# Key sums of an attention block: per-unit accumulators filled by adding DMAs, and a shared ring of PSUM banks

## The reference

```python
scores = jnp.einsum('bhsd,bhtd->bhst', q, k) / math.sqrt(HEAD_DIM)
scores = scores + _band_mask(S, scores.dtype)   # 0.1 where |s - t| <= 2
attn = jax.nn.softmax(scores, axis=-1)
out = jnp.einsum('bhst,bhtd->bhsd', attn, v)
```

## Time and profile before

| | |
|---|---|
| median of 3 runs | 4730.73 us (4729.35 to 4734.55) |
| the profiled execution, its own time | 4733.77 us |
| its span, first to last instruction | 4731.9 us |
| busy share of PE, DVE, POOL, ACT | 98%, 71%, 60%, 52% |
| mean granted clock of PE | 0.987 |
| attention stage, about | 670 to 4283 us |

### The profile page before, as it was taken

One profiled execution on the slowest core, in us unless ns is written; L12 is line 12 of the kernel. 1 busy time (PEld: TensorE's weight loads), 2 busy tenths in 40 slices (PEclk: granted clock), 3 DMA queues, 4 the chain that ended last, 5 costly groups with the idle time before them and its releaser, 6 DMA issues. The chain is left out here.

```text
span 4731.9 us, 68176 instructions
## 1 busy us (share of the span) xinstructions
PE 4630.4 (98%) x24976; PEld 2572.3 (54%) x24976; DVE 3346.7 (71%) x5663; ACT 2446.4 (52%) x4652; POOL 2820.4 (60%) x2207
## 2 busy tenths in 40 slices
PE   7999989999999999999999999999999999996999
PEld 6888844444444444444444444444444444434777
DVE  6444477777777777777777777777777777744776
ACT  2222226666666666666666666666666666661211
POOL 2111037777777777777777777777777777780000
PEclk9999979999999999999999999999999999998999
DMA  7655531112121212121212112111212121104443
GB/s 253 212 202 201 197 89 37 50 48 54 41 58 36 61 31 63 32 61 43 57 39 53 50 41 53 41 50 49 54 42 58 36 61 31 30 15 174 166 158 118
DMA packets 250862, 372.60 MB, mean 79 GB/s; under 512 B 36545, under 2 KB 103105, under 8 KB 245442
## 3 DMA queue, kind: packets, MB, share of 16 engines
q1 hardware_dynamic: 250562, 368.66, 26.2%
HBM read 211.82 MB, written 156.24 MB: 78 GB/s over the span
## 5 line engine op out<-in xcount | busy, mean ns | idle before, releaser
L699 DVE TENSOR_REDUCE part_max<-ps_m 128x1 f32<-128x512 f32 x4096 | 2547.8, 683 | 842.4 <-PE ps_m L595 840.6
L770 POOL TENSOR_TENSOR pair<-p_sb 128x512 f32<-128x512 f32 x2048 | 2565.9, 1283 | 920.6 <-ACT p_sb L687 597.0
L687 ACT ACTIVATE p_sb<-ps_s 128x512 f32<-128x512 f32 x4096 | 2114.8, 603 | 1288.4 <-PE ps_s L615 1225.2
L615 PE MATMUL ps_s<-q_st,k_st 97*128 97x512 f32 x4096 | 1728.5, 424 | 6.8 <-ACT p_sb L687 6.8
L595 PE MATMUL ps_m<-k_st,q_st 96*128 96x512 f32 x4096 | 1636.8, 403 | 21.6 <-POOL k_st L762 20.1
L615 PEld LDWEIGHTS ps_s<-q_st,k_st 97*128 97x128 f32 x4096 | 773.0, 189 | 1010.8 <-ACT p_sb L687 452.0
L629 PE MATMUL ps_o<-p_sb,v_sb 128*32 128x512 f32 x8192 | 1090.7, 605 | 0.0
L595 PEld LDWEIGHTS ps_m<-k_st,q_st 96*128 96x128 f32 x4096 | 786.2, 192 | 186.3 <-DVE part_max L699 29.2
L639 PE MATMUL ps_d<-pair,ones 128*32 128x512 f32 x4096 | 534.0, 593 | 3.8 <-POOL pair L770 3.8
L629 PEld LDWEIGHTS ps_o<-p_sb,v_sb 128*32 128x32 f32 x8192 | 161.3, 108 | 349.9 <-ACT p_sb L687 295.4
L166 POOL TENSOR_TENSOR xb<-xin,bo_row 128x2048 f32<-128x2048 f32 x16 | 75.5, 4716 | 428.1 <-DMA xin<-in_x 417.3
(11 more groups left out here) (93 smaller groups left out, 2631.9 us busy)
## 6 DMA issues: line engine op xcount, KB each, us to landing
q_st<-q_hi_d SPq DMA_DIRECT2D x128, 256.0 KB, 4.2
k_st<-k_hi_d SPq DMA_DIRECT2D x128, 256.0 KB, 4.9
xin<-in_x SPq DMA_DIRECT2D x16, 1024.0 KB, 8.4
xb_d<-xb SPq DMA_DIRECT2D x16, 1024.0 KB, 5.1
q_hi_d<-s_hi SPq DMA_DIRECT2D x64, 256.0 KB, 2.0
q_lo_d<-s_lo SPq DMA_DIRECT2D x64, 256.0 KB, 2.3
k_hi_d<-s_hi SPq DMA_DIRECT2D x64, 256.0 KB, 2.3
k_lo_d<-s_lo SPq DMA_DIRECT2D x64, 256.0 KB, 2.6
```

What stands on the lines that cost most here:

```text
L615: nc.tensor.matmul(ps_s[:, (HG * s + h) % RING_S, :], k_st[0:ROWS + 1, unit // QC % 2, kt // TT, h, kt % TT * P:(kt % TT + 1) * P], q_st[0 ...
L687: nc.scalar.activation(p_sb[:, s % SLOTS, h, :], ps_s[:, (HG * s + h) % RING_S, :], ACT.Exp, scale=SCALE).then_inc(p_ready, 1)
L699: nc.vector.tensor_reduce(part_max[:, unit % 2, col, n:n + 1], ps_m[:, seq % RING_M, :], AX.X, ALU.max).then_inc(max_taken, 1)
L770: nc.gpsimd.tensor_tensor(pair[:, m % PAIR_RING, h, :], p_sb[:, s % SLOTS, h, :], p_sb[:, (s + 1) % SLOTS, h, :], ALU.add).then_inc(paired, 1)
```

## The change

Key sums are no longer accumulated by PE for every macro. SBUF holds two accumulators (`acc`, even and odd macros) for each of two units. POOL writes the first two pair sums of a unit straight into them, one instruction of 2048 columns a macro. For each of the six later macros it adds the odd step's slot of `p_sb` to the even step's slot in place (so it first waits for that step's product with V), waits for its own result, and issues a DMA that adds the slot to the accumulator (`accum_op=ALU.add`, 1 MB). The two DMA semaphores are `merged[0]` and `merged[1]`. PE multiplies ones with the two accumulators once a unit (`add_keys(unit)`, behind step 6 of the next unit), into a bank of the maxima's ring. That ring gets the fourth bank, the former `ps_d`; `free_bank`, `max_place`, `turn_place` and `sum_place` compute whose bank is reused. The products with V of two steps now follow each other, behind each even step. ACT may overwrite an even slot only once its macro's DMA has landed. Band products of step s-1 now come behind the second take of step s, `copy_sum` before step 7, `o_high` before step 13, POOL's `scale_o` and `o_low` behind macros 4 and 5, and the SyncE chain at steps 7, 8, 10 and 11.

```diff
-    RING_S, RING_M = 3, 3
+    RING_S, RING_M = 3, 4
-    PAIR_RING = 4
+    MERGES = PAIRS // 2 - 1
+    SUM_AT = 6
+    SUM_AFTER = HG * (SUM_AT + LEAD + 1)
...
+    def sums_before(unit, j):
+        return max(unit - 2 + (j >= SUM_AFTER), 0)
+    def max_place(unit, j):
+        return max_no(unit, j) + sums_before(unit, j)
+    def sum_place(unit):
+        return max_place(unit + 2, SUM_AFTER) - 1 if unit < NU - 2 else MAXES * NU + NU + unit
+    def merges_to(m):
+        return MERGES * (m // PAIRS) + m % PAIRS // 2
...
-        pair = sb("pair", [P, PAIR_RING, HG, CH])
+        acc = sb("acc", [P, 2, 2, HG, CH])
...
         @block.sync
-                        if kt == 4:
+                        if kt == 7:
                             store_sum(unit - 1)
-                        if kt == 6:
+                        if kt == 8:
                             load_den(unit - 1)
-                        if kt == 9:
+                        if kt == 10:
                             store_rec(unit - 1)
...
         @block.tensor
+            def free_bank(place):
+                old = place - RING_M
+                if old in sum_places:
+                    pe.wait_ge(sum_copied, sum_places[old] + 1)
+                else:
+                    at_least(pe, max_taken, old + 1 - sums_to[max(old, 0)])
+                return place % RING_M
...
+            def add_keys(unit):
+                bank = free_bank(sum_place(unit))
+                for n in range(2):
+                    pe.wait_ge(merged[n], 16 * MERGES * (unit + 1))
+                    for h in range(HG):
+                        last = nc.tensor.matmul(ps_m[h * HD:(h + 1) * HD, bank, :], ones[:], acc[:, unit % 2, n, h, :],
+                                                start=(n == 0), stop=(n == 1))
                 last.then_inc(sum_done, 1)
...
-                if 2 <= s < ST + 2:
+                if s % 2 == 0 and 2 <= s < ST + 2:
                     weigh(s - 2)
-                if s >= 4 and s % 2 == 1:
-                    add_keys(s // 2 - 2)
+                    weigh(s - 1)
+                if s >= KT and s % KT == SUM_AT:
+                    add_keys(s // KT - 1)
...
         @block.scalar
-                if kt == 4 and unit > 0:
+                if kt == 7 and unit > 0:
                     copy_sum(unit - 1)
-                if kt == 14 and unit > 0:
+                if kt == 13 and unit > 0:
                     o_high(unit - 1)
                 if s >= SLOTS:
+                    old = (s - SLOTS) // 2
                     act.wait_ge(pv_done, s - SLOTS + 1)
-                    act.wait_ge(paired, HG * ((s - SLOTS) // 2 + 1))
+                    act.wait_ge(paired, old + 1)
+                    if s % 2 == 0 and old % PAIRS > 1:
+                        act.wait_ge(merged[old % 2], 16 * merges_to(old))
...
         @block.vector
             for m in range(NM):
-                if m > 0:
-                    spread_band(2 * m - 1)
                 for s in (2 * m, 2 * m + 1):
                     for h in range(HG):
                         ahead(*max_at(s, h))
-                spread_band(2 * m)
+                        if h == 1 and s > 0:
+                            spread_band(s - 1)
...
         @block.gpsimd
-                at_least(pool, sum_done, m - PAIR_RING + 1)
-                for h in range(HG):
-                    nc.gpsimd.tensor_tensor(pair[:, m % PAIR_RING, h, :], p_sb[:, s % SLOTS, h, :],
-                                            p_sb[:, (s + 1) % SLOTS, h, :], ALU.add).then_inc(paired, 1)
+                unit, n = m // PAIRS, m % PAIRS
+                p_even, p_odd, total = p_sb[:, s % SLOTS], p_sb[:, (s + 1) % SLOTS], acc[:, unit % 2, n % 2]
+                if n < 2:
+                    at_least(pool, sum_done, unit - 1)
+                    nc.gpsimd.tensor_tensor(total, p_even, p_odd, ALU.add).then_inc(paired, 1)
+                else:
+                    pool.wait_ge(pv_done, s + 1)
+                    nc.gpsimd.tensor_tensor(p_even, p_even, p_odd, ALU.add).then_inc(paired, 1)
+                    at_least(pool, merged[n % 2], 16 * (merges_to(m) - 1))
+                    pool.wait_ge(paired, m + 1)
+                    pool.dma_start(total, p_even, accum_op=ALU.add).then_inc(merged[n % 2], 16)
-                if m % PAIRS == 5 and m > PAIRS:
+                if n == 4 and unit > 0:
-                    scale_o(m // PAIRS - 1)
+                    scale_o(unit - 1)
```

More of the change, by code:

```diff
@@ L439, in attend @@
     scored, p_ready, banded, paired = sem("scored"), sem("p_ready"), sem("banded"), sem("paired")
+    merged = [sem(f"merged{i}") for i in range(2)]
     pv_done, sum_done, o_copied, sum_copied, o_out, sum_out = (
@@ L453, in attend, with max_no, turn_no, turn_place @@
     bands_to = list(itertools.accumulate(int(near(s) is not None) for s in range(ST)))
-    def max_seq(unit, j):
+    def max_no(unit, j):
         return MAXES * unit + j + (unit - 1 + (j >= TURN_AFTER) if unit else 0)
-    def turn_seq(unit):
+    def turn_no(unit):
         return MAXES * (unit + 1) + unit + (TURN_AFTER if unit < NU - 1 else 0)
+    def sums_before(unit, j):
+        return max(unit - 2 + (j >= SUM_AFTER), 0)
+    def max_place(unit, j):
+        return max_no(unit, j) + sums_before(unit, j)
+    def turn_place(unit):
+        return turn_no(unit) + (sums_before(unit + 1, TURN_AFTER) if unit < NU - 1 else NU - 2)
+    def sum_place(unit):
+        return max_place(unit + 2, SUM_AFTER) - 1 if unit < NU - 2 else MAXES * NU + NU + unit
+    sum_places = {sum_place(unit): unit for unit in range(NU)}
+    sums_to = list(itertools.accumulate(int(place in sum_places) for place in range(sum_place(NU - 1) + 1)))
     def max_at(s, m):
@@ L506, in put_shift @@
             def put_shift(unit):
-                sp.wait_ge(max_taken, turn_seq(unit) + 1)
+                sp.wait_ge(max_taken, turn_no(unit) + 1)
                 sp.dma_start(f32(q_st[ROWS:ROWS + 1, unit % QC]).rearrange("o h (t q) -> o (h t) q", q=P),
@@ L592, in maximum @@
                     pe.wait_ge(k_loaded[n], 48 * (g + 1))
-                seq = max_seq(unit, j)
-                at_least(pe, max_taken, seq - RING_M + 1)
-                nc.tensor.matmul(ps_m[:, seq % RING_M, :], q_st[0:ROWS, u, h, t * P:(t + 1) * P],
+                bank = free_bank(max_place(unit, j))
+                nc.tensor.matmul(ps_m[:, bank, :], q_st[0:ROWS, u, h, t * P:(t + 1) * P],
                                  k_st[0:ROWS, g % 2, n, h, :], start=True, stop=True).then_inc(max_scored, 1)
             def turn(unit):
-                seq = turn_seq(unit)
-                pe.wait_ge(max_taken, seq - RING_M + 1)
+                bank = free_bank(turn_place(unit))
                 pe.wait_ge(max_row, unit + 1)
-                nc.tensor.transpose(ps_m[0:HG * TT, seq % RING_M, 0:P], neg_max[:], ident[:]).then_inc(max_scored, 1)
+                nc.tensor.transpose(ps_m[0:HG * TT, bank, 0:P], neg_max[:], ident[:]).then_inc(max_scored, 1)
             def ahead(unit, j):
@@ L631, in weigh @@
                 last.then_inc(pv_done, 1)
-            def add_keys(m):
-                unit, n = m // PAIRS, m % PAIRS
-                if n == 0:
-                    at_least(pe, sum_copied, unit)
-                pe.wait_ge(paired, HG * (m + 1))
-                for h in range(HG):
-                    last = nc.tensor.matmul(ps_d[h * HD:(h + 1) * HD, :], ones[:], pair[:, m % PAIR_RING, h, :],
-                                            start=(n == 0), stop=(n == PAIRS - 1))
+            def add_keys(unit):
[5 more added lines that the diff above has]
+                                                start=(n == 0), stop=(n == 1))
                 last.then_inc(sum_done, 1)
@@ L647, in _ @@
                 ahead(1, j)
-            for s in range(ST + 4):
+            for s in range(ST + SUM_AT + 1):
                 if s < ST:
@@ L665, in copy_sum @@
             def copy_sum(unit):
-                act.wait_ge(sum_done, PAIRS * (unit + 1))
+                act.wait_ge(sum_done, unit + 1)
                 at_least(act, o_out, 32 * unit)
-                nc.scalar.activation(sum_st, ps_d[:], ACT.Copy).then_inc(sum_copied, 1)
+                nc.scalar.activation(sum_st, ps_m[:, sum_place(unit) % RING_M, :], ACT.Copy).then_inc(sum_copied, 1)
             def o_high(unit):
@@ L767, in _ @@
                     pool.wait_ge(banded, bands_to[s + 1])
-                at_least(pool, sum_done, m - PAIR_RING + 1)
-                for h in range(HG):
-                    nc.gpsimd.tensor_tensor(pair[:, m % PAIR_RING, h, :], p_sb[:, s % SLOTS, h, :],
-                                            p_sb[:, (s + 1) % SLOTS, h, :], ALU.add).then_inc(paired, 1)
-                if m % PAIRS == 5 and m > PAIRS:
-                    scale_o(m // PAIRS - 1)
-                if m % PAIRS == 6 and m > PAIRS:
-                    o_low(m // PAIRS - 1)
+                unit, n = m // PAIRS, m % PAIRS
```

(3 more changed lines are left out.)

12 lines of the change are left out of this document (5 added, 7 removed).

## The result

The changed kernel takes 5194.65 us (median of 4 runs, 5190.22 to 5205.87) against 4730.83: a ratio of 1.098, 95% interval 1.096 to 1.100. The forecast was 4507, range 4330 to 4770. Both the sign and the range are wrong.

A forecast was written before the change was run, and what follows sets the result against it. PE's own list was taken as the bound. 48.64 + 1.76 + 1.5 + 0.5 = 52.4 us a unit, 3.7 less than 56.1, over 63 periods saves 233; the tail adds 9: 4507 us, range 4330 to 4770.

The forecast's parts named there:

- PE's list: PE's matmuls in attention: blocks of 3.95, macros of 5.83, a floor of 48.64 us a unit, 7.5 less than before.
- ACT's rounding: Rounding of the output at step 13, a block's start, waiting for POOL's scaling: 0.5 us a unit.
- the small DMAs: Transfers of shift, sums and reciprocals: late only if queued behind the adding DMAs; the shift lands 2.5 before PE wants it.
- sign of being wrong: Wrong if the small DMAs' landing grows from 1.8 to over 4 us and PE waits for the shift.
- DVE's bands: Four wide band products a unit between DVE's takes delay maxima and products with V: 0.88 twice, 1.76 us a unit.
- ACT's 1.5: ACT's insertions a unit: output copy 0.5, rounding 0.5, copy of sums 0.1, exponentials' pace 0.4; together 1.5 us.
- X: Latency of one adding DMA of 1 MB from SBUF into SBUF: 8.0 us.
- d: POOL's issue of an accumulating DMA, in six macros of eight: 1.1 us.
- Rival (c): Slower: accumulating DMA as bound, from 7.6 us per MB or latency 13; at 9 us the kernel takes 5286; chance 0.19.
- 0.5 a unit for that wait: ACT's wait to overwrite a slot until its adding DMA has landed: 0.5 us a unit.
- The clock: PE's granted clock in attention after the change: still 1.00.
- rival (a): Followers' stalls vanish, bands absorbed and insertions hidden: PE's floor with the tail, near 4270, to 4360 us; chance 0.10.

The follow-up runs named there:

- c_only: Changed kernel with the unscaled output buffer doubled, so scaling and rounding have a unit more: 4878.86 us, 1.030 of the kernel before.
- a_both: Changed kernel with POOL's additions in four pieces and the reciprocals' load as four DMAs: 4962.74 us, 1.047 of the kernel before.
- c_free: c_only plus reciprocals in four DMAs, reciprocal behind step 8, bands arranged apart from POOL's additions: 4622.71 us, 0.977 of the kernel before.
- d_small: c_free with each adding DMA moving 64 KB in place of 1 MB (output not the reference's): 4517.31 us, 0.954 of the kernel before.
- p_wide: Kernel before with POOL's four additions of 512 columns made one of 2048, nothing else: 4729.88 us, ratio 0.999.
- d_floor: c_free with band products replaced by small fills and adding DMAs of 64 KB: 4273.4 us, 0.903 of the kernel before.
- d_noband: c_free with each band product replaced by a small fill: 4427.4 us, 0.936 of the kernel before.
- e_both: c_free with every band behind its own step's takes and POOL's additions in four pieces: 4737.63 us, 1.001 of the kernel before.
- b_inv: a_both with VectorE's reciprocal of the sums behind step 8's maxima in place of step 9's: 4954.74 us, 1.047 of the kernel before.
- a_rec4: Changed kernel with the broadcast load of the reciprocals as four DMAs over 32 partitions each: 5077.79 us, 1.074 of the kernel before.
- e_split: c_free with POOL's additions in four pieces of 512 columns: 4708.81 us, 0.994 of the kernel before.

## Why the prediction was wrong

**PE's list: right.** Block 3.95, burst 1.85 (1.88 forecast), macro 5.80 (5.83), unit 48.79 (48.64) where nothing else stood in the way.

**The step that failed: ACT's rounding, priced at 0.5 us.** The prediction had "POOL's scaling ends 8.2 behind burst 10, so 2.4 behind burst 12, where ACT wants it at 2.5". It followed POOL's order alone and never walked the chain that feeds the scaling: copy of the sums, store, load, reciprocal, store, a 256 KB load, scaling, rounding. The medians of the starts, counted from the first score of the unit in which they run:

| | before | changed |
|---|---|---|
| copy of the sums | 14.1 | 26.3 |
| reciprocal | 34.3 | 37.7 |
| issue of the 256 KB load | 36.0 | 44.6 |
| scaling | 46.2 | 51.2 |
| rounding | 47.7 | 52.5 |

The rounding came 4.8 later, though the change had put it one step earlier. The late sums are not what holds the reciprocal: their load goes out at 28.6 and lands 1.7 later, 7 us before the reciprocal's place in DVE's list comes. What is exposed is the way through memory behind it. The store of the reciprocals lands in 5.7 instead of 1.4, and SyncE waits for that before it issues the load. The load takes 9.7 from issue to use; in the tail of before it took 5.2 (issued at 4271.81, used at 4277.02), and inside attention the scaling stood some 10 behind it and never waited.

The prediction left all this at nothing, by the clause that the small DMAs "are late only if queued behind these". They were queued behind them, and the price of that was never worked out. Its sign of being wrong, a landing of over 4 us, came in the reciprocals' store and not in the shift, which kept its 1.8. In place of the 0.5, ACT waited 7.5 us a unit for the scaling, and c_only shows what that was worth: 316 of the 464 lost come back by making room for this chain alone.

**DVE's bands: priced 1.76 a unit at 0.69 each, a term mis-sized.** They cost 2.3 a unit on a_both, 3.1 on c_free and 3.9 on d_small; on the changed kernel itself they were not taken out. POOL's and DVE's timelines of the changed kernel show how a band gets long:

```profile
2598.52 4.58 POOL L810 TENSOR_TENSOR p_sb<-p_sb 128x2048 f32<-128x2048 f32 x1 [1.21 <-PE ps_o L663]
```
```profile
2601.07 2.59 DVE L762 TENSOR_TENSOR p_sb<-p_sb,band_f 128x520 f32<-128x520 f32 x1
2603.59 0.68 DVE L735 TENSOR_REDUCE part_max<-ps_m 128x1 f32<-128x512 f32 x1
```

The addition ends at 2603.10, the band at 2603.66, 0.56 behind it. Over all 352 bands of the changed kernel: 213 start with POOL at rest, and none of them takes over 0.70 us (mean 0.59). The other 139 take 1.96 on average; 137 of these start during an addition, a scaling or a low part, and none of the 137 ends before it. The longest, 6.75 us, starts just ahead of POOL's low part and lasts through it and the addition close behind. Takes, whose input lies in PSUM, are not held: the 1791 that lie wholly inside an addition average 0.683, the others 0.680. The Trainium skill (GPSIMD Engine Reference, section Key points) says that GpSimd contends with VectorE's instructions of two SBUF inputs; the trace agrees in the kind of instruction, and the size is from the rows. A long addition by itself does no harm: p_wide is within 0.1% of before, and bands there seldom meet it early (35 of 352 start while POOL runs, and 3 take above 1.5 us). In the changed kernel POOL starts behind the burst, just ahead of the bands. How much of the bands' price is this contention and how much their place among the takes stays open: POOL is so full in c_free that the bands still met its additions (mean 1.22).

**The rest of ACT's 1.5: not there.** d_floor has the three copies (the rounding before step 1) and ACT's pace, and is 0.15 above PE's sum.

**The adding DMA: X and d right, their cost not.** X is 8.5 in the median (8.0 forecast), d is 0.87 (1.1), with 0.55 instead of 0.1 ahead of it. An engine spends 0.492 x 3580/339 = 5.2 us on each, so the prediction's question about reading the destination is answered in between (3.1 and 6.2). Rival (c), chance 0.19, had the sign, and its time of 5286 is near, but by luck. Its mechanism, the DMAs as the bound or ACT waiting for slots, is refuted: 5.2 is under its 7.6, X under its 13, the DMA share 0.66, and ACT waited 45 us in all for slots. The prediction's 0.5 a unit for that wait was a mis-sized term all the same: once the chain has room and the bands are gone, the traffic costs 154, 2.4 a unit, and this is the wait that d_noband shows. In the changed kernel the traffic cost time mainly by slowing the small transfers of the chain, whose price the rows gave beforehand only unloaded. The estimate of 6.8 for X from the Trainium skill's two pages (DMA: Bandwidth & Descriptors, Collectives: The Full Stack), which the prediction gave beside its sum, is lower than the measured 8.5 and about the least that was seen, 6.9.

**The clock: forecast at 1.00, it was 0.91.** The page's mean is 0.916 against 0.987: the lower of the two levels is half the full clock, so (1 - 0.916) x 2 x 5192.6 = 872 us of the span were spent there, against 123 before. In e_both the mean is 0.945, in c_free 0.974. What that did to PE can be read from the windows: it is busy for 3038.20/3580 x 63.22 = 53.7 us a unit in the changed kernel and for 2870.42/2880 x 48.79 = 48.6 in d_floor, with the same matmuls. Of the 14.4 us a unit between the two, 5.0 are thus matmuls that take longer and 9.4 are idle time. The prediction had put 3.8 a unit for all stalls and nothing for the clock. How much of the 5.0 would have been waited for anyway is open: no run has the stalls without the lower clock.

**The ledger.** Changed kernel 5194.7; chain freed -316; four loads and earlier reciprocal -65; bands arranged -192; bands and traffic out -349; leaves 4273. That this is rival (a)'s 4270 does not bear (a) out, for here the bands and the traffic are taken out of the kernel and not hidden. The order of the steps decides how much each is credited with, for they interact: in b_inv the earlier reciprocal gave nothing.

## What to carry to other kernels

When a change moves the moment at which a result is complete, walk every consumer's chain from the new moment to the last instruction that waits in order on a busy engine, with DMA latencies under the new load, not those of an idle queue. Work taken off the bound engine (7.5 us a unit here) is slack taken from all its followers at once. Give a chain through memory a buffer of its own, so that nothing in the exponentials' list waits for it, before work is taken off the bound engine.

## What the runs showed of the hardware

- In these kernels an accumulating DMA of 1 MB from SBUF into SBUF lands in 8.5 us (6.9 to 14.6) and takes 5.2 us of each engine; 64 KB land in 2.4. GpSimd's issue is 0.87.
- Under them an 8 KB store to HBM lands in 5.7 instead of 1.4, and a broadcast load of 256 KB takes 9.7 (5.2 to 12.5) instead of 5.2 from issue to use. As four DMAs over 32 partitions, each lands in 4.2 and the last is used 7.7 behind the first's issue (a_rec4).
- In the changed kernel a VectorE product of two SBUF operands that starts while a GpSimd instruction on SBUF operands runs does not end before it: a wide one (128x520) ends about 0.56 us after it, one of 128x8 0.03, also through two that follow each other closely (6.75 us in one case). A VectorE reduction whose input lies in PSUM keeps its 0.68 us. GpSimd's issue of a DMA does not hold the product: in e_split 22 wide ones lie wholly inside such an issue and keep their 0.68 to 0.70.
